# Squaring q and k with one 1024-column ScalarE instruction over two PSUM banks

## The reference, cut to what matters

```python
def l2norm(t):
    return t / jnp.clip(jnp.linalg.norm(t, axis=-1, keepdims=True), 1e-12)

qkv = h @ wqkv                       # (tokens, 3 * 512)
q, k, v = jnp.split(qkv, 3, axis=-1) # each 8 heads of 64
q = l2norm(q) * qs
k = l2norm(k) * ksc
q, k = rotary_xpos(q, k)             # tables of cos and sin, by position
o = local_attention(q, k, v)         # softmax over 128 keys a query
x = x + o @ wo
```

## Time and profile before

| | |
|---|---|
| median of 3 runs | 434.38 us |
| lowest and highest | 434.32 and 435.46 us |
| span of the profiled execution | 431.7 us |
| VectorE, ScalarE, GpSimd busy | 321.6, 280.8, 301.1 us |
| TensorE busy | 351.5 us |

### The profile page before, as it was taken

How to read it: one execution, slowest core, us unless ns; L and a number is a source line. 1 busy time by engine, 2 the same in 40 slices (tenths; PEclk the granted TensorE clock), 3 DMA queues, 4 the chain that set the end, 5 groups by cost and what they waited for, 6 DMA issues and landing times.

```text
span 431.7 us, 11030 instructions
## 1 busy us (share of the span) xinstructions
PE 351.5 (81%) x3832; PEld 287.5 (67%) x3832; DVE 321.6 (74%) x751; ACT 280.8 (65%) x844; POOL 301.1 (70%) x247
## 2 busy tenths in 40 slices
PE   1573055899999899999999999999999989988781
PEld 1352034677778687778777887788778867766561
DVE  6889964787689767966796788688869877954653
ACT  3552263688678677867786788678777868764430
POOL 2200419899999889988998699869887988780222
PEclk9996557999999999999999999999999999998966
DMA  7700042412142125112511342043204220220110
GB/s 262 225 0 0 13 125 60 110 27 50 46 118 56 32 55 141 30 30 64 133 32 33 105 94 51 15 121 76 62 3 117 65 53 2 57 57 2 24 49 25
DMA packets 42373, 28.29 MB, mean 66 GB/s; under 512 B 21668, under 2 KB 36566, under 8 KB 42326
## 3 DMA queue, kind: packets, MB, share of 16 engines
q1 hardware_dynamic: 42325, 27.68, 24.4%
HBM read 13.51 MB, written 3.15 MB: 39 GB/s over the span
## 4 chain that ended last, share of the span: by engine, by line
PE 37%; DVE 23%; POOL 19%; issue 11%; ACT 7%; DMA 1%; SPq 1%; POOLq 1%; DVEq 0%; ACTq 0%
POOL rn L507 7%; PE bank L726 5%; POOL rot L552 4%; PE bank L771 4%; DVE rot_sin L1153 4%; PE upper L708 3%; DVE rot_cos L1153 3%; POOL rot L541 3%; ACT probs L902 3%; PE bank L650 2%; PE bank L763 2%; DVE normed L1052 2%; PE upper L659 2%; PE bank L590 2%; DVE neg_max L1201 2%
## 5 line engine op out<-in xcount | busy, mean ns | idle before, releaser
L902 ACT ACTIVATE probs<-upper,neg_max 128x128 f32<-128x128 f32 x256 | 90.4, 369 | 48.5 <-DVE neg_max L1201 48.4
L507 POOL TENSOR_TENSOR rn<-floored,minus_half 128x16 f32<-128x16 f32 x32 | 93.8, 2930 | 2.7
L541 POOL TENSOR_TENSOR rot<-rot_cos,rot_sin 128x512 f32<-128x512 f32 x32 | 40.9, 1277 | 44.3 <-issue 23.6
L1201 DVE TENSOR_REDUCE neg_max<-upper 128x4 f32<-128x512 f32 x64 | 43.1, 684 | 27.5 <-PE upper L708 27.4
L552 POOL TENSOR_TENSOR rot<-rot,rn 128x1024 f32<-128x1024 f32 x32 | 60.9, 1903 | 2.5
L902 ACT ACTIVATION_READ_ACCUMULATOR probs<-upper,neg_max 128x1 f32 x256 | 53.0, 207 | 0.0
L590 PE MATMUL bank<-wqkv_hi,act_t_hi 128*128 128x512 f32 x96 | 43.3, 452 | 7.9 <-DVE act_t_lo L1140 2.8
L1153 DVE TENSOR_TENSOR rot_cos<-bank,tab 128x512 f32<-128x512 f32 x64 | 43.6, 681 | 2.0 <-PE bank L594 1.9
L1153 DVE TENSOR_TENSOR rot_sin<-bank,tab 128x512 f32<-128x512 f32 x64 | 43.4, 679 | 0.0
L542 POOL TENSOR_TENSOR rot<-rot_cos,rot_sin 128x512 f32<-128x512 f32 x32 | 40.9, 1279 | 0.0
L1160 DVE TENSOR_REDUCE ss<-sq 128x16 f32<-128x1024 f32 x32 | 38.7, 1209 | 2.4 <-ACT sq L944 2.3
(11 more groups left out here) (140 smaller groups left out, 863.7 us busy)
## 6 DMA issues: line engine op xcount, KB each, us to landing
v_mid<-v_tok SPq DMA_DIRECT2D x64, 128.0 KB, 2.3
tab_raw<-tables SPq DMA_DIRECT2D x8, 512.0 KB, 3.4
h_tok<-group_in SPq DMA_DIRECT2D x14, 128.0 KB, 3.5
x_res<-group_in SPq DMA_DIRECT2D x28, 64.0 KB, 1.8
wqkv_raw<-wqkv SPq DMA_DIRECT2D x2, 768.0 KB, 6.8
x_in<-x SPq DMA_DIRECT2D x4, 256.0 KB, 3.6
head_scale<-head_scales SPq DMA_DIRECT2D x8, 128.0 KB, 4.0
group_in<-normed SPq DMA_DIRECT2D x4, 256.0 KB
```

The source lines that it names most:

```text
L507: pool.tensor_tensor(rn[:, 0:2 * HEADS], floored[:, 0:2 * HEADS], minus_half[:, :], ALU.pow).then_inc(rn_ready, 1)
L541: pool.tensor_tensor(rot[cur.par][:, :, 0:32], rot_cos[:, :, 0:32], rot_sin[:, :, 32:64], ALU.add).then_inc(rot_added, 1)
L902: last = act.activation(probs[:, h, :], s_bank[half][:, (h % 4) * P:(h % 4 + 1) * P], ACT.Exp, bias=neg_max[a.par][:, h:h + 1], accum_out= ...
L1201: dve.tensor_reduce(neg_max[a.par][:, 4 * half:4 * half + 4], src, AX.X, ALU.max, negate=True).then_inc(max_ready, 1)
```

## The change

Banks 0 and 1 become one PSUM tensor `lower` of 2 x 512 columns, at the same place. ScalarE waits for both halves of `rotate` and then squares q and k in one instruction of 1024 columns. `squared` counts once a tile instead of twice, and the waits for it follow.

```diff
-        bank = [ctx.enter_context(nc.psum_tensor(f"bank{i}", [P, 512], F32)) for i in range(4)]
+        lower = ctx.enter_context(nc.psum_tensor("lower", [P, 2, 512], F32))
+        bank = [lower[:, i, :] for i in range(2)]
+        bank += [ctx.enter_context(nc.psum_tensor(f"bank{i}", [P, 512], F32)) for i in (2, 3)]
...
-                need(pe, squared, 2 * a.t)
+                need(pe, squared, a.t)
...
-                        pe.wait_ge(squared, 2 * taken)
+                        pe.wait_ge(squared, taken)
...
-                        for n, (b, read) in enumerate(((q_bank, q_rot), (k_bank, k_rot))):
-                            act.wait_ge(read, 2 * (cur.t + 1))
-                            act.activation(sq[:, n * INNER:(n + 1) * INNER], b[:, :], ACT.Square).then_inc(squared, 1)
+                        act.wait_ge(q_rot, 2 * (cur.t + 1))
+                        act.wait_ge(k_rot, 2 * (cur.t + 1))
+                        act.activation(sq[:, :].rearrange("p (b d) -> p b d", b=2), lower[:, :, :], ACT.Square).then_inc(squared, 1)
...
-                dve.wait_ge(squared, 2 * (a.t + 1))
+                dve.wait_ge(squared, a.t + 1)
```

## The result

| | before | after |
|---|---|---|
| median of 16 runs each | 433.70 us | 435.86 us |
| lowest and highest | 432.08, 435.95 us | 434.16, 438.72 us |
| ratio, 95% interval | 1 | 1.0058 (1.0038 to 1.0078) |
| span of the profiled execution | 431.7 us | 436.3 us |

What follows compares the result with a forecast made beforehand. The chain was read as shared by TensorE, VectorE and GpSimd, ScalarE having 7%. Terms -0.17 + 0.43 + 0.15 + 0.14 + 0.05 + 0.04 + 0.04 + 0.07 = +0.75 us on 434.38 gave 435.1; 8-in-10 range 433.8 to 437.4.

Steps and rivals of the forecast that it cites:

- The rival by which ScalarE's saving counts: ScalarE's queue decides, so each tile saves 0.11 us, at most 3.5 us in all: 430.9; chance 0.07.
- The dearer instruction: Two banks cost a second start: 0.54 instead of 0.43 at about eight places, 436.1 us; chance 0.08.
- The delays of steps 8, 12, ..., 28: mix_values moves by 0.43 us there, counted as nothing because covered; rival that the cover fails: 437.7 us, chance 0.20.
- the tie of 0.01 us: After step 16: next rotation delayed to 225.90, while TensorE waits until 225.91 for GpSimd anyway, so nothing was counted.
- the path of the feed-forward part over GpSimd: After the covered steps, the feed-forward part's way leads over GpSimd's next power and not over ScalarE.
- the slack of steps 7, 10, 11 and 14: Copy-to-mix_values distance above 0.63 us, taken to absorb delay: 0.28 in step 7, 0.30 in step 14.
- +0.15 (step 7): Step 7: distance 0.91 us, slack 0.28 against a delay of 0.43, leaving +0.15 us.
- +0.14 (steps 10 and 11 together): Steps 10 and 11: taken to behave like step 14, adding +0.14 us.
- +0.05 (what step 14 leaves after step 15): Step 14 passes on 0.13 us; with 0.43 more against step 15's slack of 0.51, +0.05 us is left.
- 0.43 us: In 29 steps the square of k starts as before but ends 1.03 - 0.60 = 0.43 us later.
- The -0.17 us of steps 0 and 2: Both banks are free when ScalarE comes, so the merged square ends earlier: -0.06 in step 0, -0.11 in step 2.
- within 0.3%: Outcome "same", 433.1 to 435.7 us: chance 0.62, against 0.31 for slower and 0.07 for faster.

Runs made afterwards that it cites:

- e1: Kernel before, still two 512-column squares, but both placed behind the waits for q and for k; ratio to before 1.0095.
- e3: Changed kernel with ScalarE's copy (save_probs) put ahead of the 1024-column square; ratio to before 0.9986.
- e8: Changed kernel with the copy ahead of the square and the wait for k_rot riding on the square; ratio to before 0.9996.
- e5: Changed kernel with TensorE's wait for the copy last of the four waits ahead of mix_values, in the hardware loop only; ratio to before 1.0063.
- e7: Changed kernel with the square's same three waits reordered so that the wait for k_rot rides on the square; ratio to before 1.0066.
- e4: Changed kernel without the wait for q_rot ahead of the wait for k_rot; ratio to before 1.0062.
- e9: Changed kernel with both wait orders: k_rot riding on the square, and the copy's wait last ahead of mix_values in steps 7 to 14; ratio to before 0.9996.

## Why the prediction was right in its mechanism and too small in its size

**Right.** The square of k was held by `rot_sin` of k and not by ScalarE, so merging loses the head start; the square takes 1.03 us (32 at 1027 ns); the delay goes by way of the copy into `mix_values` (e1 and e3 show both ends). The rival by which ScalarE's saving counts is out: e8 keeps the saving and is no faster. The dearer instruction is out: e1 has none and is slower. The delays of steps 8, 12, ..., 28 are covered, as forecast: `mix_values` of step 16 moved by 3.23 us and GpSimd's addition by 2.72 in step 16, 2.73 in step 17 and 2.75 in step 18. But it was not the tie of 0.01 us that covered them. `mix_values` of step 17 moved by 2.94, so 0.2 us got past the tie. What hid it is the path of the feed-forward part over GpSimd, which the prediction also named: the addition of step 17 waits for VectorE's `h`, in the kernel before and in the changed one.

```profile
228.86 1.27 POOL L541 TENSOR_TENSOR rot<-rot_cos,rot_sin 128x512 f32<-128x512 f32 x1 [1.44 <-DVE h L1177]
```

```profile
231.59 1.27 POOL L543 TENSOR_TENSOR rot<-rot_cos,rot_sin 128x512 f32<-128x512 f32 x1 [1.44 <-DVE h L1179]
```

**Wrong: the slack of steps 7, 10, 11 and 14.** The prediction took 0.63 us as the least distance between copy and `mix_values` everywhere, from steps 3 and 16, and read the 0.91 to 0.93 of steps 7 and 14 as 0.28 to 0.30 us of slack. But steps 7 to 14 run in the hardware loop, and in steps 7, 10, 11 and 14 0.91 to 0.92 is the least: three more waits stand between. The terms +0.15 (step 7), +0.14 (steps 10 and 11 together) and +0.05 (what step 14 leaves after step 15) measured +0.48, +0.49 and +0.34 together, and +0.48. From the addition of step 6 to that of step 18 it was 1.82 us in place of 0.34. e5 takes 0.99 of them back. This is the larger error, and a sign of it stood in the trace of the kernel before: in its chain of waits "issue", and not the copy, comes just ahead of `mix_values` in step 7, 0.11 us of it.

```profile
124.09 0.44 PE upper L659 x4
124.53 0.11 issue
124.64 1.15 PE bank L726 x32
```

**Wrong: 0.43 us.** The prediction had the squares start 0.03 to 0.04 us after `rot_sin` of k as before, but the merge also moved the wait for k from the square onto an instruction ahead of it: 0.094 to 0.116 us, and the copy 0.48 to 0.51 later. Where slack is nearly used up the difference comes through whole: +0.12 in step 19 in place of 0.04, and +0.07 in steps 18 and 22, for which the prediction has no term. So the groups from step 16 to 20 and from 20 to 24 grew by 0.21 us each, where the prediction had them unchanged within 0.1. e7 shows what the later start is worth: 0.79 us from step 3 to 31.

**The start of the layers.** The -0.17 us of steps 0 and 2 are not in the profile of the changed kernel, whose clock from 62 to 104 us is 0.85 and not 0.90. In e4, whose start matches the kernel before to 0.01 us, the addition of step 2 comes 0.18 us earlier and that of step 3 0.11 earlier; its clock is 0.91, so how much of this is the merge stays open.

**What is left.** Up to `mix_values` of step 31 the forecast's terms sum to 0.92 us from step 3 on, and e9, with both errors put right, has 1.2 us more than the kernel before there (381.86 - 90.08 = 291.78 against 379.30 - 88.75 = 290.55 us). The surplus of 0.3 us lies between steps 6 and 18, 0.61 us in place of 0.34, where the least distance is 0.72 in most steps of the loop and the forecast has 0.63. Outside of it the terms came out: step 3 +0.42 for 0.43, steps 19 and 23 +0.05 for 0.04. The 1.32 us of the table is higher because the addition of step 31 still carries a part of step 30's delay, which the slack of step 31 takes back.

**The time.** The forecast put "within 0.3%" first and the time at 435.1; the ratio is 1.0058, in the part that was given 0.31. That 435.1 lies within 0.8 us of the measured 435.86 is in part luck: the 434.38 it starts from is 0.7 us above the median of more runs, and the change itself was forecast at 0.75 us and measured at 2.2. The price of the dearer instruction, 436.1, lies nearer still, and that rival is excluded.

## What to carry to other kernels

Two instructions that each wait for their own half overlap the wait; one instruction over both starts when the last half is ready. Before merging, look at what the second one's start follows: a semaphore, or the first one's end, even where the engine shows no idle time. And count the slack of a wait from a step of the same form: in a hardware loop the waits queued behind the late one are part of the distance, and in the traces it paid to let the wait that ends last be the one that rides on the instruction (e5 and e7, 0.99 and 0.79 us of 289; the times don't resolve it).

## What the runs showed of the hardware

- A wait for a semaphore that stands as an instruction of its own ahead of ScalarE's square costs 0.06 us over one that rides on it (0.094 against 0.034 from the end of `rot_sin`). Where the instruction of its own holds two waits it is 0.08 (0.116). Which of them rides depends on the order in the program, in the loop and outside of it differently (e4, e7).
- Three waits behind the decisive one cost TensorE 0.28 us in steps 7 and 11 of the loop (0.91 against 0.63, e5).
- One square over two PSUM banks takes 1.03 us, as 512 columns more at 0.835 ns each; the second bank costs nothing. By the Trainium skill, "ScalarE: Activation LUTs", section "What ACT_TABLE_LOAD costs", an estimate is 1.04 us for it and 1.13 for the pair: the measured 1.03 and 1.09 (e1) are near it. The Trainium skill, "Advanced Engine Details and Errata", section "TRN2 Errata", advises large tiles and names one instruction over several banks as a way. Here that cost 0.58% while the instruction stood behind the later wait on the way to the copy, and with the copy put ahead it cost nothing and gained nothing (e3, e8).
